# Output projection in segment 3 instead of segment 4 of every step, and ScalarE's copy of p ahead of its copy of k in odd steps

## The chip, the cores and the metric

The kernel runs on one core of a Trainium2 chip. The metric is the device time of one execution in microseconds (us); lower is better. TensorE is called PE, and PEld is its weight load; VectorE is DVE, ScalarE is ACT, GpSimd is POOL and SyncE is SP. SP issues all the DMAs.

## What is computed

One transformer layer on x of shape 16 x 512 x 256 in float32: x = x + attention(layernorm(x)), then x = x + ffn(layernorm(x)).

```python
qkv = inputs @ W_qkv                        # 256 -> 2048 (q), 1024 (k), 1024 (v)
# 32 query heads of 64, 16 key/value heads, each shared by two query heads
scores = einsum('bhqd,bhkd->bhqk', q, k) / 8 + slope[h] * (k_pos - q_pos)
attn = softmax(where(q_pos >= k_pos, scores, -inf))
out = einsum('bhqk,bhkd->bhqd', attn, v).reshape(B, S, 2048) @ W_out
# ffn, low rank: 256 -> 64 -> 1024, gelu, 1024 -> 64 -> 256
P = x @ U1;  H = gelu(P @ V1 + b1);  Q = H @ U2;  y = Q @ V2 + b2
```

## The kernel before

**Precision.** Each operand of a large product is kept as two float16 parts, a high and a low half, and a product is three matmuls (`split_mm`, L547). ACT writes most high halves (function `copy`, L812), DVE most low halves (`low`, L984), POOL the low half of p and of o (L1284, L1303).

**Passes, steps, segments.** The batch has 16 sequences. Each engine runs one instruction stream over passes i = 0 to 17 (modes FIRST for 0, MID for 1 to 15, LAST and TAIL for the emptying of the pipeline). A pass has 16 steps s, one for each key/value head, and a step has 5 segments n. The work is a software pipeline: in step s of a pass, q and k are projected for head s, the row maxima are taken for head s - 2, scores and exponentials belong to head s - 7, the attention products to head s - 8, and the rows of o of head s - 9 are transposed. So pass i still finishes sequence i in the first half of the steps of pass i + 1.

**PE, in each segment, in program order** (loop at L757 on): `scores(s, n)`; in four steps of a pass the FFN's `ffn_h`; `max_scores(s, n)`; in segments (15, 3) and (15, 4) the transposes of the next x; in segment 0 of odd steps the projection of k; in segment 4 the output projection `project_out` (L672); in segment 1 (even steps) or 2 (odd steps, and step 0) the projection of q; in segments 1 and 3 one of the two attention products, `attend(s, 0)` and `attend(s, 1)`, "the first" and "the second product" in what follows; in segment 4 of steps 0 to 3 and 8 to 11 the projection of v; and smaller pieces of the FFN. PE starts its operations in this order. Two PSUM banks serve the scores, so `scores(s, n)` waits for the exponential of two segments before, and two serve the maxima.

**The output projection.** o_t has room for 8 heads and is read in groups of 4 heads. Steps 12 to 15 project heads 0 to 3 (128 tokens in each step), steps 0 to 3 heads 4 to 7, steps 4 to 7 heads 8 to 11, steps 8 to 11 heads 12 to 15. Each is 12 matmuls of 128x128 by 256 columns. At the first step of a group (12, 0, 4, 8) `project_out` waits for the transposes of all its four heads. The last of those is issued by SP in that same step: SP waits for `lo_o`, which POOL gives at L1303 in segment 0, after ACT's `o_hi_lo` copy (in segment 0, behind the exponential of that segment and, where there is one, the copy of v), which waits for DVE's `o_f` (L1100) from the second product of the step before.

```python
def project_out(s):
    group, t = out_use(s)
    bank = next_proj(("out", s), acc_done, 16 * i + s - OUT_LAG + 1)
    if t == 0:
        for slot in range(2):
            pe.wait_ge(ot_in[slot], at(16 * (8 * i + (s - OUT_LAG) // 2 + 2)))
```

**DVE** adds the projected rows in `residual(s)` (L1053; the instruction is L1050), in the same segment as `project_out`; in steps 8 to 11 `statistics(s)` of the second layernorm follows. In segments 1 and 3 `normalise` (L1095, L1100) comes near the end of the segment's work.

**ACT** takes in segment n the copy of p of segment n - 1 (`high_p`, "the copy of p"), then the exponential of segment n (L862), and then the rest: v, o, maxima, k (`high_k`, L875) in segment 0 of odd steps, and layernorm pieces. In segment 1 of steps 13, 15, 1 and 3 it also computes two GELUs (L964), with a table load before and after them.

**PSUM banks of the projections.** Three banks are handed out in turn over the uses listed by `projection_order()`; `next_proj` makes PE wait until the use of three places before has been read.

Of the kernel before, what the change touches and what calls it, by code (L numbers as in the profile page):

```python
# [32 lines left out]
T = S // P  # L33
# [31 lines left out]
MAX_SEG, K_SEG, V_SEG, O_SEG = 2, 0, 4, 4  # L65
# [5 lines left out]
OUT_RING, OUT_GROUP, OUT_LAG, OUT_SEG = 8, 4, 12, 4  # L71
# [44 lines left out]
    return divmod(SEG * s + n - lag, SEG)  # L116


def q_segment(s):

    return 2 if s % 2 or s == 0 else 1
# [21 lines left out]
def projection_order():  # L143

    uses = []
    for s in range(KV):
        for n in range(SEG):
            if (s, n) in H_PAIRS:
                uses += [("h", 2 * H_PAIRS[s, n]), ("h", 2 * H_PAIRS[s, n] + 1)]
            if n == MAX_SEG and s % 4 == 2:  # L150
                uses.append(("max", s))
            if (s, n) in X_PAIRS:
                uses.append(("x", X_PAIRS[s, n]))
            if n == K_SEG and s % 2 == 1:
                uses.append(("k", s))
            if n == OUT_SEG:
                uses.append(("out", s))
            if (s, n) in LN2_T_AT:
                uses.append(("ln2", LN2_T_AT[s, n]))
            if n == q_segment(s):  # L160
                uses.append(("q", s))
                if s in SKIP_BANK:
                    uses.append(("skip", s))
            if n == V_SEG and s % 8 < 4:
                uses.append(("v", s))
            if (s, n) in U1_AT:
                uses.append(("p", U1_AT[s, n]))
            if (s, n) == Y_AT:
                uses += [("y", 0), ("y", 1)]
            if (s, n) in U2_PAIRS:  # L170
                uses.append(("u", U2_PAIRS[s, n]))
    return uses
# [12 lines left out]
FIRST, MID, LAST, TAIL = "first", "mid", "last", "tail"  # L185


def steps(mode):

    return range(STORE_AT + 1) if mode == TAIL else range(KV)  # L190
# [40 lines left out]
def out_in(mode, s):  # L231

    return mode in (FIRST, MID) if s >= OUT_LAG else mode in (MID, LAST)


def p_place(s, n):

    return (SEG * (s - ATT) + n) % P_RING


def in_stage(mode, s, lag):

    return s >= lag if mode == FIRST else s < lag if mode == LAST else mode == MID


def layer(nc, x, w_qkv, w_out, u1, v1, b1, u2, v2, b2, k_aug, q_aug, ident_d, ident_b_d, causal_d, out):
    B = x.shape[0]
    ctx = ExitStack()
    with ctx:
# [141 lines left out]
        def ffn_batch(i, s):  # L391

            return i - 1 if s >= 8 else i - 2

        def ffn_in(i, s):

            return 0 <= ffn_batch(i, s).value() < B
# [5 lines left out]
        def h_pairs(i, s):  # L403
            return {} if not ffn_in(i, s) else END_H_PAIRS if at_end(ffn_batch(i, s)) else H_PAIRS
# [4 lines left out]
        def u2_pairs(i, s):  # L409
            return {} if not ffn_in(i, s) else END_U2_PAIRS if at_end(ffn_batch(i, s)) else U2_PAIRS  # L410
# [126 lines left out]
        def _(pe):  # L537
# [30 lines left out]
            def body(i, mode):  # L568
# [189 lines left out]
                for s in steps(mode):  # L758
                    if mode == FIRST and s == 2:

                        pe.wait_ge(k_rows, 2)
                    if mode == FIRST and s == 6:
                        pe.wait_ge(const_in, 64)
                    if mode == FIRST and s == 8:
                        pe.wait_ge(set_done, 1)
                    if mode == FIRST and s == OUT_LAG:
                        pe.wait_ge(wo_lo, 2)
                    for n in range(SEG):
                        if in_stage(mode, s, ATT):
                            scores(s, n)  # L770
                        if (s, n) in h_pairs(i, s):
                            ffn_h(ffn_batch(i, s), h_pairs(i, s)[s, n])
                        if n == MAX_SEG and s % 4 == 2 and in_stage(mode, s, 6):
                            transpose_max(s)
                        if in_stage(mode, s, 2):
                            max_scores(s, n)
                        if (s, n) in X_PAIRS and mode in (FIRST, MID):
                            pair = X_PAIRS[s, n]
                            next_proj(("x", pair), lo_ln1, 2 * (i + 1) + pair + 1)
                            transpose_x(i + 1, pair)  # L780
                        if n == K_SEG and s % 2 == 1 and mode in (FIRST, MID):
                            pair = (s - 1) // 2
                            project(next_proj(("k", s), lo_k, i * (KV // 2) + pair + 1), QD + pair * P, pe_k)
                        if n == OUT_SEG and mode == LAST and s == OUT_LAG - T:
                            project_out_end()
                        elif n == OUT_SEG and out_in(mode, s) and not (mode == LAST and s > OUT_LAG - T):
                            project_out(s)
                        if n == q_segment(s) and mode in (FIRST, MID):
                            if s == 0:
                                pe.wait_ge(lo_ln1, at(2 * (i + 1)))  # L790
                            project(next_proj(("q", s), lo_q, i * KV + s + 1), s * P, pe_q)
                        if n in (1, 3) and in_stage(mode, s, ATT + 1):
                            attend(s, n // 2)
                        if (s, n) in LN2_T_AT and mode != FIRST:
                            transpose_x2(LN2_T_AT[s, n])
                        if n == V_SEG and s % 8 < 4 and mode in (FIRST, MID):
                            project_v(s)
                        if (s, n) in U1_AT and mode != FIRST:
                            ffn_p(U1_AT[s, n])
                        if (s, n) == Y_AT and ffn_in(i, s):  # L800
                            ffn_y(ffn_batch(i, s), 0)
                            ffn_y(ffn_batch(i, s), 1)
                        if (s, n) in u2_pairs(i, s):
                            ffn_u2(ffn_batch(i, s), u2_pairs(i, s)[s, n])
# [5 lines left out]
        def _(act):  # L810
# [41 lines left out]
            def body(i, mode):  # L852
# [11 lines left out]
                def high_p(s, n):  # L864
                    a = i * KV + s - ATT
                    if (s % KV, n) in POOL_MASKS:
                        act.wait_ge(masked, mask_count(i, s, n))
                    else:
                        act.wait_ge(exp_done, at(SEG * a + n + 1))

                    if 2 * a + AV_BEFORE[n] > 0:
                        act.wait_ge(pe_av, at(2 * a + AV_BEFORE[n]))
                    copy(p_hi[:, p_place(s, n), :], p_f[:, n, :]).then_inc(hi_p, 1)

                def high_k(s):  # L875
                    act.wait_ge(pe_k, at(i * (KV // 2) + (s + 1) // 2))
                    landed = K_DMAS * 16 * (2 * i + (s - 3) // RING + 1)
                    if landed > 0:
                        act.wait_ge(kdup_in[(s - 3) % RING // 2], at(landed))
                    copy(ks[0][:, :], proj("k", s)[:, :], KV_OUT).then_inc(hi_k, 1)  # L880
# [9 lines left out]
                for s in steps(mode):  # L890
# [4 lines left out]
                    for n in range(SEG):  # L895
# [4 lines left out]

                        if n > 0 and in_stage(mode, s, ATT):
                            high_p(s, n - 1)
                        if n == 0 and in_stage(mode, s, ATT + 1):
                            high_p(s - 1, SEG - 1)
                        if before(s, n, PP_LAG) in U1_AT and mode != FIRST:
# [28 lines left out]
                        if n == MAX_SEG and s % 4 == 2 and in_stage(mode, s, 6):  # L934
# [4 lines left out]
                            if 32 * (2 * i + q4 // 2 + 1) > 0:  # L939
                                act.wait_ge(m_in[q4 % 2], at(32 * (2 * i + q4 // 2 + 1)))  # L940
                            copy(mt[0][:, :], proj("max", s)[0:8 * T, 0:P], -1.0).then_inc(hi_m, 1)
                        if n == K_SEG and s % 2 == 1 and mode in (FIRST, MID):
                            high_k(s)
                        if (s, n) in LN1_AT and mode in (FIRST, MID):
                            t = LN1_AT[s, n]
                            if t == 0:
# [34 lines left out]
        def _(dve):  # L981
# [46 lines left out]
            def body(i, mode):  # L1028
# [75 lines left out]
                for s in steps(mode):  # L1104
# [3 lines left out]
                    for n in range(SEG):  # L1108
# [27 lines left out]
                        if n == q_segment(s) + q_lag(s) and mode in (FIRST, MID):  # L1136
                            dve.wait_ge(hi_q, at(g + 1))
                            low(qs[1][:, s % 2, :], proj("q", s)[:, :], qs[0][:, s % 2, :], Q_OUT).then_inc(lo_q, 1)
                        if n == OUT_SEG and out_in(mode, s):
                            if mode == LAST and s >= OUT_LAG - T:  # L1140
                                if s == OUT_LAG - T:
                                    dve.wait_ge(acc_done, at(16 * i - T))
                                    for k in range(T):
                                        residual(s + k)
                                    for k in range(T):
                                        statistics(s + k)
                            else:
                                residual(s)
                                if s in range(OUT_LAG - T, OUT_LAG) and mode != FIRST:
                                    statistics(s)  # L1150
# [233 lines left out]
```

## Time and profile before

| | |
|---|---|
| median of 3 runs | 2745.33 us (2740.84 to 2749.11) |
| profiled execution, its time | 2744.49 us |
| its span in the trace | 2742.5 us |
| mean granted TensorE clock | 0.989 |
| PE busy | 96% |
| POOL, ACT, DVE busy | 79%, 78%, 74% |

The span is what the trace covers, from the first to the last instruction; the time of the execution lies 2 us above it. In the stretch between the first and the last pass the schedule repeats every 165 us, once for each sequence. Times within the trace are counted from the start of the span.

### The profile page before, as it was taken

Reading aid. Unit: us, or ns where it says so; the run is one execution under the profiler, and the core shown is the slowest. Engines: PE = TensorE matmul, PEld = TensorE weight load, DVE = VectorE, ACT = ScalarE, POOL = GpSimd, SP = SyncE. Lnnn points to the kernel's source line nnn. Section 1 sums busy time; section 2 is a strip of 40 time slices with the busy share of each in tenths; the row PEclk is TensorE's granted clock in tenths of the full one; section 3 lists DMA queues with packets and bytes.
Section 4 is the critical chain, followed back from the end, with each engine's and each line's share of the span. In section 5 each row is a group of like instructions: output and inputs, shape, how many; then the busy total and the mean of one; then the engine's idle time right before and its main releaser. Section 6 shows DMA issues by size and latency. Waiting matters only on the chain.

```text
span 2742.5 us, 83206 instructions
## 1 busy us (share of the span) xinstructions
PE 2634.9 (96%) x30344; PEld 1797.7 (66%) x30344; DVE 2033.6 (74%) x6857; ACT 2142.4 (78%) x3856; POOL 2170.4 (79%) x2221
## 2 busy tenths in 40 slices
PE   5999999999999999999999999999999999999985
PEld 2666666666666667666666666666666666666663
DVE  5677777777777778777787777778777787777753
ACT  4777878778787887878778788877878778787883
POOL 4878788787877878788887887878788787887884
PEclk8999999999999999999999999999999999999997
DMA  6444444444445445444444444444444444444421
GB/s 182 100 98 96 97 95 93 96 94 93 98 91 105 93 89 103 95 94 97 96 94 94 95 92 98 98 92 95 94 102 94 93 101 89 99 96 95 99 46 32
DMA packets 489112, 260.75 MB, mean 95 GB/s; under 512 B 310064, under 2 KB 485168, under 8 KB 488704
## 3 DMA queue, kind: packets, MB, share of 16 engines
q1 hardware_dynamic: 488704, 255.44, 44.8%
q8 instruction: 241, 3.95, 0.6%
q14 instruction: 167, 1.37, 0.2%
HBM read 27.73 MB, written 8.39 MB: 13 GB/s over the span
## 4 chain that ended last, share of the span: by engine, by line
PE 68%; ACT 11%; issue 9%; POOL 5%; DVE 3%; DMA 2%; SPq 1%; ACTq 0%; POOLq 0%; DVEq 0%
PE proj L544 33%; PE scores L544 16%; PE o_acc L544 11%; PE max_scores L544 7%; ACT p_f L862 3%; ACT L862 3%; POOL p_lo L1284 3%; ACT p_hi L812 2%; ACT h_f L964 2%; POOL o_hi_lo L1303 1%; DMA o_t<-o_hi_lo 1%; DMA q_operands<-neg_max_t_lo 1%; POOL p_f L1278 1%; DVE max_scores L1043 1%; POOL h_lo L1289 1%
## 5 line engine op out<-in xcount | busy, mean ns | idle before, releaser
L1284 POOL TENSOR_TENSOR p_lo<-p_f,p_hi 128x512 f16<-128x512 f32 x1280 | 1477.4, 1164 | 249.5 <-ACT p_hi L812 248.0
L1043 DVE CUSTOM_DVE_ANT_0 max_scores<-max_scores,causal 128x512 f32<-128x512 f32 (+3 forms) x2048 | 971.4, 506 | 238.8 <-PE max_scores L544 201.7
L812 ACT ACTIVATE p_hi<-p_f 128x512 f16<-128x512 f32 x1280 | 804.7, 629 | 208.3 <-POOL p_f L1278 197.2
L862 ACT ACTIVATE p_f<-scores 128x512 f32<-128x512 f32 x1280 | 756.5, 591 | 176.0 <-PE scores L544 146.0
L544 PE MATMUL scores<-q_operands,k_lo_hi 128*128 128x512 f16 (+3 forms) x2048 | 607.5, 300 | 32.8 <-ACT p_f L862 26.1
L544 PE MATMUL scores<-q_operands,k_hi_aug 128*128 128x512 f16 (+3 forms) x2048 | 565.2, 299 | 0.0
L544 PE MATMUL o_acc<-v_hi_one,p_lo 128*128 128x65 f16 x5120 | 517.5, 194 | 15.7 <-POOL p_lo L1284 12.4
L544 PE MATMUL o_acc<-v_hi_one,p_hi 128*128 128x65 f16 x5120 | 517.0, 194 | 0.0
L544 PE MATMUL o_acc<-v_lo,p_hi 128*128 128x64 f16 x5120 | 516.4, 193 | 0.0
L544 PE MATMUL max_scores<-k_hi_aug,q_operands 96*128 96x512 f16 (+3 forms) x2048 | 492.1, 302 | 14.0 <-DMA k_lo_hi<-k_pair_lo 9.0
L544 PEld LDWEIGHTS o_acc<-v_hi_one,p_lo 128*128 128x128 f16 x5120 | 470.5, 98 | 50.5 <-POOL p_lo L1284 25.1
L544 PEld LDWEIGHTS o_acc<-v_lo,p_hi 128*128 128x128 f16 x5120 | 468.1, 98 | 39.5
L544 PEld LDWEIGHTS o_acc<-v_hi_one,p_hi 128*128 128x128 f16 x5120 | 467.4, 97 | 0.0
L1303 POOL TENSOR_TENSOR o_hi_lo<-o_f,o_hi_lo 128x512 f16<-128x512 f32 x256 | 296.9, 1160 | 171.3 <-ACT o_hi_lo L812 171.3
L544 PE MATMUL proj<-wo_hi,o_t 128*128 128x256 f16 x2016 | 372.7, 273 | 5.1 <-DMA o_t<-o_hi_lo 5.1
L544 PE MATMUL proj<-xn_t_hi,wqkv_lo 128*128 128x512 f16 x768 | 294.5, 383 | 3.2 <-DVE k_pair_lo L984 1.7
L544 PE MATMUL proj<-xn_t_lo,wqkv_hi 128*128 128x512 f16 x768 | 293.9, 383 | 0.0
L544 PE MATMUL proj<-xn_t_hi,wqkv_hi 128*128 128x512 f16 x768 | 293.8, 383 | 0.0
L544 PEld LDWEIGHTS scores<-q_operands,k_lo_hi 128*128 128x128 f16 x2048 | 199.8, 98 | 134.9 <-ACT p_f L862 35.1
L1043 DVE DVE_READ_ACCUMULATOR2_ANT row_max<- 128x1 f32 x2048 | 282.1, 138 | 1.3
L544 PE MATMUL scores<-ident_bf,causal 128*128 128x128 bf16 x1280 | 280.3, 219 | 0.0
L544 PE MATMUL proj<-wo_lo,o_t 128*128 128x256 f16 x1008 | 274.8, 273 | 0.0
(134 smaller groups left out, 4409.4 us busy)
## 6 DMA issues: line engine op xcount, KB each, us to landing
q_operands<-q_pair_hi SPq DMA_DIRECT2D x512, 128.0 KB, 2.5
q_operands<-q_pair_lo SPq DMA_DIRECT2D x512, 64.0 KB, 2.0
k_hi_aug<-k_pair_hi SPq DMA_DIRECT2D x256, 64.0 KB, 2.0
k_lo_hi<-k_pair_hi SPq DMA_DIRECT2D x256, 64.0 KB, 2.0
k_lo_hi<-k_pair_lo SPq DMA_DIRECT2D x256, 64.0 KB, 2.0
x_rows<-in_L_attn_inputs SPq DMA_DIRECT2D x17, 512.0 KB, 4.1
x_acc<-in_L_attn_inputs SPq DMA_DIRECT2D x64, 128.0 KB, 2.4
out<-x_rows SPq DMA_DIRECT2D x16, 512.0 KB, 3.4
```

The costliest lines, as they stand in the source:

```text
L544: return nc.tensor.matmul(out_ap, lhs, rhs, start=start, stop=stop, skip_group_check=True)
L812: return nc.scalar.activation(out_ap, in_ap, ACT.Copy, scale=scale)
L862: nc.scalar.activation(p_f[:, n, :], score_bank[(SEG * s + n) % 2][:, :], ACT.Exp).then_inc(exp_done, 1)
L964: nc.scalar.activation(h_f[:, c % 2, :], h_place(f, c)[:, :], ACT.Gelu_apprx_tanh, bias=b1c[:, c:c + 1], scale=1.0 / FFN_SCALE).then_inc(g ...
L1043: last = nc.vector.tensor_tensor_reduce(out=bank, in0=bank, in1=causal[:, (T - 1 - qt) * P:S], scale=1.0, scalar=-3e38, op0=ALU.add, op1=A ...
L1278: nc.gpsimd.affine_select(both, both, [[0, 2], [1, P]], ALU.is_ge, 0.0, base=0, channel_multiplier=-1).then_inc(masked, 1)
L1284: nc.gpsimd.tensor_tensor(p_lo[:, place, :], p_f[:, n, :], p_hi[:, place, :], ALU.subtract).then_inc(lo_p, 1)
L1289: nc.gpsimd.tensor_tensor(h_lo[:, c % 2, :], h_f[:, c % 2, :], h_hi[:, c % 2, :], ALU.subtract).then_inc(lo_h, 1)
L1303: nc.gpsimd.tensor_tensor(o_hl[:, slot, 1, :], o_f[:, slot, :, :].rearrange("p t c -> p (t c)"), o_hl[:, slot, 0, :], ALU.subtract).then_i ...
```

## The change

`OUT_SEG` is 4, and a new function `out_segment(s)` gives 3 for every step. PE's order and DVE's (`residual`, `statistics`) both take it, and so does the list from which the PSUM banks of the projections are handed out. Within segment 3, PE's code has the output projection ahead of the attention product, and DVE's has `residual` ahead of `normalise`. On ACT `high_k` moves from the end of segment 0 to segment 1, behind the copy of p that opens that segment and ahead of its exponential.

```diff
--- before.py
+++ after.py
@@ -116,6 +116,11 @@
     return divmod(SEG * s + n - lag, SEG)
 
 
+def out_segment(s):
+
+    return OUT_SEG - 1
+
+
 def q_segment(s):
 
     return 2 if s % 2 or s == 0 else 1
@@ -153,7 +158,7 @@
                 uses.append(("x", X_PAIRS[s, n]))
             if n == K_SEG and s % 2 == 1:
                 uses.append(("k", s))
-            if n == OUT_SEG:
+            if n == out_segment(s):
                 uses.append(("out", s))
             if (s, n) in LN2_T_AT:
                 uses.append(("ln2", LN2_T_AT[s, n]))
@@ -781,9 +786,9 @@
                         if n == K_SEG and s % 2 == 1 and mode in (FIRST, MID):
                             pair = (s - 1) // 2
                             project(next_proj(("k", s), lo_k, i * (KV // 2) + pair + 1), QD + pair * P, pe_k)
-                        if n == OUT_SEG and mode == LAST and s == OUT_LAG - T:
+                        if n == out_segment(s) and mode == LAST and s == OUT_LAG - T:
                             project_out_end()
-                        elif n == OUT_SEG and out_in(mode, s) and not (mode == LAST and s > OUT_LAG - T):
+                        elif n == out_segment(s) and out_in(mode, s) and not (mode == LAST and s > OUT_LAG - T):
                             project_out(s)
                         if n == q_segment(s) and mode in (FIRST, MID):
                             if s == 0:
@@ -900,6 +905,8 @@
 
                         if n > 0 and in_stage(mode, s, ATT):
                             high_p(s, n - 1)
+                        if n == K_SEG + 1 and s % 2 == 1 and mode in (FIRST, MID):
+                            high_k(s)
                         if n == 0 and in_stage(mode, s, ATT + 1):
                             high_p(s - 1, SEG - 1)
                         if before(s, n, PP_LAG) in U1_AT and mode != FIRST:
@@ -939,8 +946,6 @@
                             if 32 * (2 * i + q4 // 2 + 1) > 0:
                                 act.wait_ge(m_in[q4 % 2], at(32 * (2 * i + q4 // 2 + 1)))
                             copy(mt[0][:, :], proj("max", s)[0:8 * T, 0:P], -1.0).then_inc(hi_m, 1)
-                        if n == K_SEG and s % 2 == 1 and mode in (FIRST, MID):
-                            high_k(s)
                         if (s, n) in LN1_AT and mode in (FIRST, MID):
                             t = LN1_AT[s, n]
                             if t == 0:
@@ -1136,7 +1141,7 @@
                         if n == q_segment(s) + q_lag(s) and mode in (FIRST, MID):
                             dve.wait_ge(hi_q, at(g + 1))
                             low(qs[1][:, s % 2, :], proj("q", s)[:, :], qs[0][:, s % 2, :], Q_OUT).then_inc(lo_q, 1)
-                        if n == OUT_SEG and out_in(mode, s):
+                        if n == out_segment(s) and out_in(mode, s):
                             if mode == LAST and s >= OUT_LAG - T:
                                 if s == OUT_LAG - T:
                                     dve.wait_ge(acc_done, at(16 * i - T))
```

## Rows read from the trace of the kernel before

**Rows 1.** The profile's page, part 1: busy us, share of the span, instructions.
```profile
PE 2634.9 (96%) x30344; PEld 1797.7 (66%) x30344; DVE 2033.6 (74%) x6857; ACT 2142.4 (78%) x3856; POOL 2170.4 (79%) x2221
```

**Rows 2.** Waits, 440 to 2420 us, of PE and PEld: total us, times, longest.
```profile
PEld scores L544 <- ACT p_f L862: 23.6, 48, 0.6
...
PE scores L544 <- ACT p_f L862: 17.2, 36, 0.5
...
PE proj L544 <- DMA o_t<-o_hi_lo: 3.8, 4, 1.3
...
PE o_acc L544 <- POOL p_lo L1284: 3.4, 12, 0.3
```

**Rows 3.** Timeline, step 8: start us, us, engine, line, operation, out<-in, [idle before <-releaser].
```profile
1384.71 0.62 ACT L812 ACTIVATE o_hi_lo<-o_f 128x512 f16<-128x512 f32 x1
...
1385.41 1.16 POOL L1303 TENSOR_TENSOR o_hi_lo<-o_f,o_hi_lo 128x512 f16<-128x512 f32 x1 [0.72 <-ACT o_hi_lo L812]
...
1386.65 1.25 SPq L488 DMA_TRANSPOSE o_t<-o_hi_lo  x1
...
1388.46 0.19 PE L544 MATMUL o_acc<-v_hi_one,p_lo 128*128 128x65 f16 x1
...
1389.37 0.27 PE L544 MATMUL scores<-q_operands,k_lo_hi 128*128 128x256 f16 x1
...
1390.03 0.27 PE L544 MATMUL proj<-wo_hi,o_t 128*128 128x256 f16 x1
...
1391.34 0.38 PE L544 MATMUL proj<-wqkv_hi,xn_t_lo 128*128 128x512 f16 x1
```

**Rows 4.** Tile o_t over the whole span: time from issue to landing.
```profile
DMA to landing us min/median/max: 3.0/3.1/6.5
```

**Rows 5.** Timeline at step 4 of the second pass: a transpose, and the projection behind it.
```profile
195.41 1.24 SPq L488 DMA_TRANSPOSE o_t<-o_hi_lo  x1
...
198.72 0.27 PE L544 MATMUL proj<-wo_hi,o_t 128*128 128x256 f16 x1 [0.28 <-DMA o_t<-o_hi_lo]
```

**Rows 6.** Tile o_t, window 195 to 200 us: that transpose's landing.
```profile
DMA to landing us min/median/max: 3.2/3.2/3.2
```

**Rows 7.** Timeline: transpose issue and start of second product, steps 0, 4, 12, 12.
```profile
1304.11 1.25 SPq L488 DMA_TRANSPOSE o_t<-o_hi_lo  x1
...
1306.73 0.19 PE L544 MATMUL o_acc<-v_hi_one,p_lo 128*128 128x65 f16 x1
...
1349.97 1.24 SPq L488 DMA_TRANSPOSE o_t<-o_hi_lo  x1
...
1351.27 0.19 PE L544 MATMUL o_acc<-v_hi_one,p_lo 128*128 128x65 f16 x1
...
1428.74 1.26 SPq L488 DMA_TRANSPOSE o_t<-o_hi_lo  x1
...
1430.27 0.19 PE L544 MATMUL o_acc<-v_hi_one,p_lo 128*128 128x65 f16 x1
...
2586.18 1.26 SPq L488 DMA_TRANSPOSE o_t<-o_hi_lo  x1
...
2587.71 0.19 PE L544 MATMUL o_acc<-v_hi_one,p_lo 128*128 128x65 f16 x1
```

**Rows 8.** Timeline of GELU steps 15 and 3: ScalarE's k, second product, next scores.
```profile
1291.75 0.60 ACT L812 ACTIVATE k_pair_hi<-proj 128x512 f16<-128x512 f32 x1 [0.40 <-PE proj L544]
...
1297.31 0.19 PE L544 MATMUL o_acc<-v_hi_one,p_lo 128*128 128x65 f16 x1
...
1298.42 0.28 PE L544 MATMUL scores<-q_operands,k_lo_hi 128*128 128x256 f16 x1
...
1341.41 0.20 PE L544 MATMUL o_acc<-v_hi_one,p_lo 128*128 128x65 f16 x1
...
1342.96 0.28 PE L544 MATMUL scores<-q_operands,k_lo_hi 128*128 128x256 f16 x1 [0.47 <-ACT p_f L862]
```

**Rows 9.** Timeline, step 0: the first product behind step 15's last p.
```profile
1302.95 0.20 PE L544 MATMUL o_acc<-v_hi_one,p_lo 128*128 128x65 f16 x1 [0.28 <-POOL p_lo L1284]
```

## The prediction

> **What bounds the kernel.** I read the page first: PE is busy 96% of the span, the others at most 79% [rows 1]. So the time changes by what PE does more, or waits more. Then the waits of PE over twelve repetitions (440 to 2420 us), to see what interrupts it: scores wait for the exponential 36 times as matmuls and 48 times as weight loads, three and four times a sequence; the output projection waits for the transposes 4 times in all; the first product waits for p's low half 12 times, once a sequence [rows 2]. PE has little idle time to win, and its order is nearly free of waits because each operand arrives just before its use. The question is what the new order wins at the first kind of wait and loses at the second. For that I read the timeline around single steps.
>
> **The move costs no PE work.** In step 8 the second product starts at 1388.46, the next scores at 1389.37, the output projection at 1390.03 and the projection of v at 1391.34 [rows 3]. So the product takes 0.91 us of PE's time and the projection 1.31 us. After the change the projection starts where the product starts now, and the product and the scores of segment 4 come 1.31 us later; from segment 4's end on the order is the old one. The same 12 matmuls, the same DVE additions and the same DMAs are issued; only waits change.
>
> **What it wins: the GELU steps.** In step 3 the scores behind the second product start 1.55 us after it (1341.41 to 1342.96), against 0.91 us in step 8: 0.64 us lost, put down to ACT, which is late by its table loads [rows 3, 8]. Steps 1 and 13 show the same (these are the 36 waits of matmuls, three a sequence [rows 2]). In step 15 the distance is 1.11 us (1297.31 to 1298.42), 0.20 us lost [rows 8]. The projection, 1.31 us ahead of the product, gives ACT that much more time and covers all four: 3 x 0.64 + 0.20 = 2.12 us a sequence.
>
> **What it costs: the first step of each group.** In steps 12, 0, 4 and 8 the projection needs a transpose issued in that very step. From issue to landing the median is 3.1 us [rows 4]. One place shows the whole wait: issued at 195.41, landed 3.2 us later [rows 6], that is at 198.61, and PE's projection starts at 198.72 with the DMA as its releaser [rows 5]. So PE starts about 0.1 us after landing, or 3.2 us after the issue in the usual case. In step 8 the issue is at 1386.65: operands are usable at 1389.85, and the projection starts at 1390.03, 0.18 us later, without a wait [rows 3]. The new place is 1388.46, which is 1.39 us too early. In the same way [rows 7]:
> - step 12: 1428.74 + 3.2 - 1430.27 = 1.67 us short
> - step 4: 1349.97 + 3.2 - 1351.27 = 1.90 us
> - step 0: 1304.11 + 3.2 - 1306.73 = 0.58 us
>
> Together 5.54 us a sequence. The pattern is the same in every sequence: the last step 12 has the issue 1.53 us ahead of the product (2586.18 and 2587.71), as the one at 1428.74 has [rows 7]. Does the issue move with the change? It hangs on ACT's copy of o (1384.71), then on POOL (1385.41, 1.16 us), then SP at 1386.65 [rows 3]. That copy stands behind the exponential of segment 0, and this one follows scores(s, 0), ahead of which PE has done the same work as before. So the issue keeps its distance to PE's schedule, where ACT is ready. The wait cannot hide behind the product any more, since PE takes its matmuls in order: what stands behind the waiting projection is the second product, then segment 4, and everyone who waits for them (DVE's normalise, ACT's exponential).
>
> **Chain behind the later scores.** The scores of segment 4 come 1.31 us later, and the path from them over exponential, copy of p and POOL's low half to the next step's first product loses the projection as cover. The same path from the scores of segment 3 does not. Three places:
> - Step 7 into step 8: no projection of v stands between, so ACT reaches the exponential of segment 0 and the copy of o later. The copies on ACT and the subtraction on POOL cost 0.62 and 1.16 us [rows 3]. I take 0.5 us on the issue in step 8; the bounds are 0 (ACT has slack) and 1.31 us (the whole shift).
> - Step 15 into step 0: the first product already waits 0.28 us for p's low half [rows 9], and DVE has the x copies to do behind a normalise that comes 1.31 us later. I take 0.3 us, bounds 0 and 1.31 us.
> - The other steps without a v projection (4 to 6 and 12 to 14) have a projection of q or k, another 1.31 us (the same 6 x 512 columns as v's), in between. I take 0.2 us in all; bounds -0.3 us (the present waits of this kind, one a sequence, might go [rows 2]) and 1.5 us.
>
> That is 1.0 us a sequence.
>
> **The k part.** ACT's copy of k waits for PE's k projection for 0.40 us in step 15 [rows 8]; the copy of p now runs in that time, and p's low half and the exponential of segment 1 get up to 0.4 us earlier. In other odd steps k's high half is later by up to one copy, 0.62 us [rows 3], and so are DVE's low half and SP's six k DMAs behind it, and on SP the odd step's transpose. Their reader is max_scores of the next step, a whole step after the k projection, and that work is its cover; in odd steps no group of the output projection starts. On PE I cost it at nothing: it is not PE's wait. Without that cover it would be 0.6 us in eight steps, 5 us a sequence. A gain is possible only through ACT's lateness in GELU steps, which the projection already covers.
>
> **The bank rotation** changes with the order. I went through the 78 uses: each waits for the use three places before, and nowhere is that a use which is read after the place where PE now asks for it. The closest are the projections of steps 13, 15, 1 and 3 behind a GELU, which is over before the second product. Nothing.
>
> **A rule against the row.** The wait rests on 3.1 us from issue to landing [rows 4]. The Trainium skill, page "DMA: Bandwidth & Descriptors", section "Anatomy of one DMA", gives a DMA a fixed cost of about 2.0 us, of the software-issued kind. As an estimate by that page, the sum would come out near no change (the second rival below). The trace does not agree, since its median for this transpose is 3.1 us.
>
> **The sum.** Per sequence: 5.54 + 1.0 - 2.12 = 4.42 us. Fifteen passes have all of it: 66.3 us. The first pass has one group start (step 12), 1.67 us. The pass that empties the pipeline has two (steps 0 and 4), and its PE is less loaded; I take 3 us, bounds 0 and 6. Together 71 us, on the profiled execution's 2744.5 us: 2815 us. That execution is 0.8 us below the median of the runs, which changes nothing here.
>
> **Rivals.**
> 1. *The waits are not there, the GELU gain is* (faster). If ACT reached the copy of o earlier in steps 12, 0, 4 and 8, the issue could come before PE needs it. What decides is whether the four waits sum to less than about 1.1 us a sequence. Then 15 x 2.12 = 32 us are won: 2713 us. For it: the GELU waits are real, 36 of them [rows 2]. Against it: the issues would have to come 1.4 to 1.9 us earlier in three steps, and their origin is PE's own scores in segment 0. Chance 0.05.
> 2. *Landing is quicker for the early reader, by 1.1 us* (no change). The four shortfalls would be 0.57, 0.80, 0.29 and 0 us, 1.66 in all; 1.66 + 1.0 - 2.12 = 0.54 us a sequence, 8 us, and with the ends 2755 us. (The Trainium skill's page "DMA: Bandwidth & Descriptors" would have it so.) Against: the minimum of all 256 landings is 3.0 us [rows 4]. Together with other ways in which shortfall and gain meet, chance 0.05.
> 3. *The chain behind the scores of segment 4 becomes the bound in all steps without v* (slower still). If eight steps lose 0.5 us each in place of my 0.2 in all, 3.8 us a sequence more: 57 us, 2872 us. For it: POOL and ACT are near 80% busy [rows 1]. Against: the q or k projection of 1.31 us still stands there. Chance 0.15.
>
> The forecast itself has 0.75. A measurement of this kernel can tell about 0.3%, 8 us, from no change. Forecast and rival 3 are slower, 0.90; rival 2 is the same, 0.05; rival 1 faster, 0.05. **Range.** With waits at 5.14 (no 0.1 us of start) and no chain term: 3.0 us a sequence, 2744.5 + 45 + 2 = 2792; a little below that if the issue moves up with ACT's relief, 2778. Up: chain terms of 3 us a sequence give 6.4, which is 96 + 5 us: 2846; I take 2850. This leaves out most of rival 3, and rivals 1 and 2.
>
> **What the profile after would show.** PE waiting for the o_t DMA four times a sequence in place of 4 times in twelve sequences, by 0.5 to 2 us, with PE's projection 3.2 us behind SP's issue in steps 12, 0, 4, 8; the waits of scores on the exponential in the GELU steps gone; the schedule repeating every 169 to 170 us in place of 165 ((2586.18 - 1428.74) / 7 [rows 7]). The forecast is wrong if the output projection of these steps starts without a wait, if GELU waits stay, or if the first product's waits for p's low half grow past 1 us a sequence.

## The result and the profile after

| | before | after |
|---|---|---|
| median of the runs | 2743.41 us (4 runs) | 2853.58 us (4 runs, 2848.98 to 2861.01) |
| ratio | | 1.0398, 95% interval 1.0383 to 1.0413 |
| span of the profiled execution | 2742.5 us | 2847.0 us |
| PE busy | 2634.9 us, 96% | 2643.6 us, 93% |
| mean granted TensorE clock | 0.989 | 0.989 |

The change costs 110 us, 4.0%. The direction was forecast; the size was forecast as 71 us, with 2850 us as the end of the range. The time lies 3.6 us above that end.

The page of the kernel after: part 1, then part 4, the chain that ended last, by engine and by line.

```profile
PE 2643.6 (93%) x30344; PEld 1791.6 (63%) x30344; DVE 2105.6 (74%) x6857; ACT 2128.0 (75%) x3856; POOL 2179.8 (77%) x2221
...
PE 69%; POOL 8%; DMA 8%; ACT 7%; issue 5%; DVE 3%; SPq 1%; ACTq 0%; POOLq 0%; DVEq 0%
...
PE proj L549 34%; PE scores L549 15%; PE o_acc L549 13%; DMA o_t<-o_hi_lo 7%; PE max_scores L549 6%; POOL p_lo L1289 4%; POOL o_hi_lo L1308 3%; ACT p_f L867 2%; ACT p_hi L817 1%; ACT o_hi_lo L817 1%; ACT L867 1%; DVE x_rows L1182 1%; PE proj L711 1%; ACT h_f L969 1%; DVE max_scores L1048 0%
```

PE is busy for about as long as before (8.7 us more) and the span of the profiled execution is 104.5 us longer: the time went into PE's waits. The DMA of o_t is 7% of the chain now; it was 1% before.

The waits of PE and PEld from 440 to 2420 us (total us, times, longest), as in [rows 2]:

```profile
PEld max_scores L549 <- DVE row_max L1048: 24.9, 57, 0.8
...
PEld scores L549 <- ACT p_f L867: 9.2, 33, 0.3
...
PE proj L549 <- DMA o_t<-o_hi_lo: 62.1, 46, 1.9
...
PE proj L549 <- DVE q_pair_lo L989: 15.2, 11, 1.4
...
PE max_scores L549 <- DVE row_max L1048: 8.8, 23, 0.4
...
PE o_acc L549 <- POOL p_lo L1289: 5.2, 11, 0.5
...
PE proj L549 <- DVE x2n_t_lo L989: 3.0, 12, 0.3
```

The stretch holds twelve sequences before and eleven and a half after. The projection waits for the transposes 46 times in place of 4. The scores wait for the exponential 33 times by at most 0.3 us as weight loads, and no more as matmuls; before it was 48 times by up to 0.6 us, and 36 of these as matmuls. Three more kinds of wait are new or grown. The projection waits 11 times for VectorE's low half of q, once a sequence and by 1.4 us each, which was not there before. A product of the FFN waits once a sequence for VectorE's `x2n_t_lo`, 0.3 us. And the maxima's products wait for VectorE: 57 weight loads do, but only 23 matmuls. Where a weight load alone waits, PE still has matmuls to finish, so the row of the matmuls, 8.8 us, is the one that counts as time of PE. The kernel before has no row of max_scores matmuls waiting for VectorE, and this one of weight loads:

```profile
PEld max_scores L544 <- DVE row_max L1043: 6.5, 24, 0.3
```

Timeline of the kernel after at the four group starts, steps 4, 8, 12 and 0: SP's transpose, PE's last max_scores ahead of the projection, and the projection.

```profile
1398.43 1.24 SPq L493 DMA_TRANSPOSE o_t<-o_hi_lo  x1
...
1399.53 0.38 PE L549 MATMUL max_scores<-k_hi_aug,q_operands 96*128 96x512 f16 x1
...
1401.63 0.27 PE L549 MATMUL proj<-wo_hi,o_t 128*128 128x256 f16 x1 [1.72 <-DMA o_t<-o_hi_lo]
...
1440.00 1.25 SPq L493 DMA_TRANSPOSE o_t<-o_hi_lo  x1
...
1441.13 0.38 PE L549 MATMUL max_scores<-k_hi_aug,q_operands 96*128 96x512 f16 x1
...
1443.21 0.27 PE L549 MATMUL proj<-wo_hi,o_t 128*128 128x256 f16 x1 [1.70 <-DMA o_t<-o_hi_lo]
...
1483.46 1.26 SPq L493 DMA_TRANSPOSE o_t<-o_hi_lo  x1
...
1484.77 0.38 PE L549 MATMUL max_scores<-k_hi_aug,q_operands 96*128 96x512 f16 x1
...
1486.70 0.27 PE L549 MATMUL proj<-wo_hi,o_t 128*128 128x256 f16 x1 [1.55 <-DMA o_t<-o_hi_lo]
...
1524.76 1.25 SPq L493 DMA_TRANSPOSE o_t<-o_hi_lo  x1
...
1527.15 0.38 PE L549 MATMUL max_scores<-k_hi_aug,q_operands 96*128 96x512 f16 x1
...
1527.96 0.27 PE L549 MATMUL proj<-wo_hi,o_t 128*128 128x256 f16 x1 [0.43 <-DMA o_t<-o_hi_lo]
```

The projection starts 3.20, 3.21, 3.24 and 3.20 us after the issue. The max_scores block ahead of it takes 0.22 us of PE (512 columns: the distance from one such matmul to the next), so PE stood 1.88, 1.86, 1.71 and 0.59 us: 6.04 us a sequence. Over all sequences the medians are 1.89, 1.85, 1.70 and 0.59 us.

Timeline of step 6, PE and DVE; the first line is the same place one sequence earlier:

```profile
1252.42 0.28 PE L549 MATMUL proj<-wo_hi,o_t 128*128 128x256 f16 x1 [1.38 <-DVE q_pair_lo L989]
...
1422.10 0.38 PE L549 MATMUL max_scores<-k_hi_aug,q_operands 96*128 96x512 f16 x1
...
1423.13 0.67 DVE L989 SCALAR_TENSOR_TENSOR q_pair_lo<-proj,q_pair_hi 128x512 f16<-128x512 f32 x1
...
1423.86 0.28 PE L549 MATMUL proj<-wo_hi,o_t 128*128 128x256 f16 x1 [1.38 <-DVE q_pair_lo L989]
```

PE is through with the maxima at 1422.32 and starts the projection at 1423.86, 1.54 us later, when VectorE's `q_pair_lo` of this step is done. The projection does not read q; it is given the PSUM bank that q has just had. The distance from 1252.42 to 1423.86 is one period of the new schedule: 171.4 us, against 165.3 us between the issues of [rows 7]. Over fifteen periods, from the maxima's transpose in step 2 of the second pass to that of the pass that empties the pipeline, the mean is 171.2 us (179.01 to 2747.25 in the trace after) against 164.6 us (175.79 to 2645.16 before): 6.6 us more a sequence, 98.9 us of the 104.5.

Timeline of GELU step 3 after, second product and next scores:

```profile
1391.85 0.19 PE L549 MATMUL o_acc<-v_hi_one,p_lo 128*128 128x65 f16 x1
...
1392.76 0.27 PE L549 MATMUL scores<-q_operands,k_lo_hi 128*128 128x256 f16 x1
```

0.91 us, where it was 1.55 us [rows 8]: the GELU wait is gone.

### The profile page after: what moved, and what is told of

It is laid out like the page before. It is cut to its first block, busy times and chain, and to the rows that moved or that the text cites. A ratio compares the mean times of both kernels' runs of the same rounds, so it can differ in the third digit from the quotient of the medians.

```text
span 2847.0 us, 83206 instructions
## 1 busy us (share of the span) xinstructions
PE 2643.6 (93%) x30344; PEld 1791.6 (63%) x30344; DVE 2105.6 (74%) x6857; ACT 2128.0 (75%) x3856; POOL 2179.8 (77%) x2221
## 4 chain that ended last, share of the span: by engine, by line
PE 69%; POOL 8%; DMA 8%; ACT 7%; issue 5%; DVE 3%; SPq 1%; ACTq 0%; POOLq 0%; DVEq 0%
PE proj L549 34%; PE scores L549 15%; PE o_acc L549 13%; DMA o_t<-o_hi_lo 7%; PE max_scores L549 6%; POOL p_lo L1289 4%; POOL o_hi_lo L1308 3%; ACT p_f L867 2%; ACT p_hi L817 1%; ACT o_hi_lo L817 1%; ACT L867 1%; DVE x_rows L1182 1%; PE proj L711 1%; ACT h_f L969 1%; DVE max_scores L1048 0%
## 5 line engine op out<-in xcount | busy, mean ns | idle before, releaser
L1283 POOL TENSOR_SCALAR_AFFINE_SELECT p_f<-p_f 128x256 f32<-128x256 f32 x384 | 157.4, 410 | 207.4 <-ACT p_f L867 201.9
L549 PEld LDWEIGHTS proj<-wo_hi,o_t 128*128 128x128 f16 x2016 | 196.5, 97 | 152.3 <-issue 105.1
```

The source lines that it names most:

```text
L549: return nc.tensor.matmul(out_ap, lhs, rhs, start=start, stop=stop, skip_group_check=True)
L1283: nc.gpsimd.affine_select(both, both, [[0, 2], [1, P]], ALU.is_ge, 0.0, base=0, channel_multiplier=-1).then_inc(masked, 1)
```

## The experiments

Two theories stood against each other. The first: the loss is the sum of single waits at places that can be named (the transposes at the four group starts, the bank in step 6, VectorE's maxima behind steps 5 and 15), less the GELU waits. The second: the loss is the lost cover between the scores of segment 4 and the next step's first product, in every step that moves, and PE's waits only stand where that lateness shows. Each kernel is timed together with the kernel before on its own chip, and the ratios are to that one. The medians of the kernel before differ by up to 4 us between the chips (2743.41 to 2747.50 us), so a few us between runs of different chips say little; e1 to e4 share a chip, e5 to e8 another, e9 and e10 a third.

### e1: the output projection alone

```diff
-                        if n == K_SEG + 1 and s % 2 == 1 and mode in (FIRST, MID):
-                            high_k(s)
                         if n == 0 and in_stage(mode, s, ATT + 1):
                             high_p(s - 1, SEG - 1)
...
+                        if n == K_SEG and s % 2 == 1 and mode in (FIRST, MID):
+                            high_k(s)
                         if (s, n) in LN1_AT and mode in (FIRST, MID):
```

> The output projection moves in all sixteen steps, ScalarE's copy of k stays where it was before. Theory (waits for the transposes 6.0 us a sequence, a bank wait of 1.5 us in step 6, some chain cost, less 2.1 us of GELU waits): the k part is worth nothing on PE, so 2853 us within 5 us. Rival (the later copy of k makes VectorE late, and that is the part of the loss that the prediction lacked, 30 to 40 us): about 2815 to 2825 us.

Measured: 2861.86 us, ratio 1.0410 (1.0393 to 1.0427). That is 4 us above the end of what was expected (2858 us), and far from the rival's. The interval overlaps the whole change's (1.0383 to 1.0413), so inside the whole change the k part is worth nothing that these times tell from zero, and it is not the missing loss. The trace does show a small share of it: with the projection alone one wait of a scores matmul a sequence is left, which the whole change does not have.

```profile
PE scores L549 <- ACT p_f L867: 3.2, 12, 0.3
```

### e2: the k part alone

```diff
 def out_segment(s):
 
-    return OUT_SEG - 1
+    return OUT_SEG
```

> Only ScalarE's copy of p goes ahead of its copy of k; the output projection stays in segment 4. Theory: no PE wait is added, and the four GELU waits of a sequence (0.64 us three times, 0.20 us) can shrink by at most the 0.40 us that the copy of p now hides, so 2725 to 2743 us. Rival (k arrives late for VectorE and the DMAs): slower than 2750 us.

Measured: 2718.04 us, ratio 0.9894 (0.9878 to 0.9909): 29 us faster, 7 us below what was expected. The waits, weight loads of the scores from 440 to 2420 us:

```profile
PEld scores L549 <- ACT p_f L867: 2.3, 13, 0.2
```

13 in place of 48. The timeline of its step 3, ACT's copy of k, PE's second product and the next scores:

```profile
1484.86 0.59 ACT L817 ACTIVATE k_pair_hi<-proj 128x512 f16<-128x512 f32 x1
...
1489.96 0.19 PE L549 MATMUL o_acc<-v_hi_one,p_lo 128*128 128x65 f16 x1
...
1491.00 0.28 PE L549 MATMUL scores<-q_operands,k_lo_hi 128*128 128x256 f16 x1
```

From product to scores is 1.04 us, 0.13 us over 0.91, where it was 0.64 us over. So 0.51 us is won in such a step: the 0.40 us that ACT waited for PE, and 0.1 us that the expectation did not count. Read in every sequence, the median distance is 1.04 to 1.05 us in steps 13, 1 and 3 (it was 1.55 us), and 0.92 us in step 15 (it was 1.11 us), so 1.7 us a sequence are won, 27 us in sixteen. The k part, costed at nothing on PE, is nearly the whole of what the kernel can win; with the projection moved it only has less to win, because the projection covers the same waits.

### e3: another bank in step 6

```diff
             if n == q_segment(s):
+                if s == 6:
+                    uses.append(("skip", s))
                 uses.append(("q", s))
-                if s in SKIP_BANK:
+                if s in SKIP_BANK[1:]:
                     uses.append(("skip", s))
```

> The whole change, but the unused place of step 6 in the rotation of the PSUM banks stands ahead of q's use and not behind it, so that step 6's output projection gets a bank other than the one q has just had. Theory: the wait of 1.54 us a sequence on VectorE's low half of q is gone, fifteen to sixteen times, 23 us less: about 2830 us. Rival (VectorE and ScalarE are late there in any case, and PE waits for something else a little later): no difference, 2850 us or more.

Measured: 2835.64 us, ratio 1.0321 (1.0305 to 1.0336): 18 us less than the whole change (21 us by the ratios, the two having run on different chips), where 23 us were expected. Waits of PEld and PE from 440 to 2420 us:

```profile
PEld max_scores L551 <- DVE row_max L1050: 25.2, 58, 0.8
...
PE proj L551 <- DMA o_t<-o_hi_lo: 64.3, 47, 2.4
```

There is no row of the projection waiting for `q_pair_lo` any more, and the waits for the transposes are a little longer (64.3 us against 62.1 us). So the bank wait was real and most of it additional. It does not come from a shifted rotation: in the list of uses of the kernel before, step 6's projection stands three places behind q of step 6 too, and has the same bank. There it came a segment later, when VectorE had read q. It is the earlier start that meets the reader, and another rotation is a remedy.

### e4: the group starts stay in segment 4

```diff
 def out_segment(s):
 
-    return OUT_SEG - 1
+    return OUT_SEG if s % OUT_GROUP == 0 else OUT_SEG - 1
```

This is on e3's rotation.

> As the run with the other bank rotation, but the first step of each group of the output projection (12, 0, 4, 8) keeps it in segment 4; the other twelve steps have it in segment 3. Theory: all waits for the transposes are gone, the GELU gain of 2.1 us a sequence stays, a chain cost of 0 to 0.5 us a sequence remains: 2712 to 2722 us, faster than the kernel before. Rival (the loss is the lost cover between the scores of segment 4 and the next first product, in every step): 12 of 16 steps keep it, so slower than the kernel before, 2770 us or more.

Measured: 2732.26 us, ratio 0.9947 (0.9932 to 0.9961). With twelve of sixteen steps moved the kernel is faster than before, so the second theory falls as the main cause: 103 us between e3 and e4 belong to the four group starts. But it is 10 us above the end of the expected range and 14 us slower than e2, which moves none. (e4 also has the other rotation, which no run has alone.) Waits of PEld and PE from 440 to 2420 us:

```profile
PEld max_scores L551 <- DVE row_max L1050: 26.1, 60, 0.8
...
PE max_scores L551 <- DVE row_max L1050: 9.2, 24, 0.4
...
PE proj L551 <- DMA o_t<-o_hi_lo: 4.1, 6, 1.5
```

The transposes are back at a few waits, and the maxima wait as much as after the whole change; e2 has no such row of matmuls. The row is two waits and 0.8 us a sequence, most of the 14 us. Where they wait is seen in the timeline of the kernel after behind step 5, DVE and PE:

```profile
1415.30 1.35 DVE L1182 SCALAR_TENSOR_TENSOR x_rows<-proj,x_rows 128x512 f32<-128x512 f32 x2 [0.44 <-PE proj L549]
...
1417.66 0.33 DVE L1048 CUSTOM_DVE_ANT_0 max_scores<-max_scores,causal 128x128 f32<-128x128 f32 x1
...
1418.10 0.39 PE L549 MATMUL max_scores<-k_hi_aug,q_operands 96*128 96x384 f16 x2 [0.33 <-DVE row_max L1048]
```

In step 5 DVE adds y (two instructions, 1415.30 to 1416.65) and normalises only after that; its maxima of segment 4 end at 1417.99, and PE's max_scores that needs their bank starts at 1418.10. PE has come to it early, because the projection that used to stand between is now ahead. The other such wait of a sequence is behind step 15.

### e5: steps 5 and 15 stay too

```diff
-    return OUT_SEG if s % OUT_GROUP == 0 else OUT_SEG - 1
+    return OUT_SEG if s % OUT_GROUP == 0 or s in (5, 15) else OUT_SEG - 1
```

> As e4, and steps 5 and 15 keep the output projection in segment 4 too; ten steps have it in segment 3. Theory: the only wait that e4 added beside e2 is PE's maxima of the next step waiting for VectorE, behind steps 5 (its y additions) and 15 (its x copies), 1.1 us a sequence; without it 17 us less than e4: 2712 to 2718 us. Rival (a cost spread over all the steps whose later scores lose the cover): at most 4 us less than e4, 2728 us or more.

Measured: 2722.47 us, ratio 0.9913 (0.9897 to 0.9930), 10 us less than e4, between the two expectations.

```profile
PEld max_scores L551 <- DVE row_max L1050: 12.9, 49, 0.3
...
PE proj L551 <- DMA o_t<-o_hi_lo: 8.1, 9, 1.8
```

The 24 waits of the maxima's matmuls are gone with the two steps: e5 has no such row. Of the weight loads 49 short waits are left, against 24 before the change, and no matmul waits behind them. So the two steps carry all that the maxima cost PE. The profile also has 9 waits for the transposes where e4 and e2 have 6, so it happened to catch more late landings (8.1 us, 5.5 us in e2), and the first product waits 3.3 us for p's low half (0.9 us in e2). That is room for the 4 us by which e5 stays above e2; whether they come from the other ten steps, from chance or from the rotation is not shown.

### e6: only the group starts move

```diff
-    return OUT_SEG - 1
+    return OUT_SEG - 1 if s % OUT_GROUP == 0 else OUT_SEG
```

> Only the four group starts (steps 12, 0, 4, 8) have the output projection in segment 3, with ScalarE's k behind p as in e2. Theory: four waits for the transposes, 6.0 us a sequence on e2's 2718 us: 2805 to 2815 us. Rival (the waits only take the place of others): less than 40 us on e2, under 2760 us.

Measured: 2822.70 us, ratio 1.0277 (1.0256 to 1.0299), 105 us above e2 and 8 us above the end of the expected range. Waits from 440 to 2420 us, then one of its steps 8:

```profile
PE proj L549 <- DMA o_t<-o_hi_lo: 66.3, 47, 2.7
...
PE o_acc L549 <- POOL p_lo L1289: 5.7, 12, 0.5
...
PE proj L549 <- DVE x2n_t_lo L989: 3.1, 12, 0.3
```

```profile
1255.76 1.25 SPq L493 DMA_TRANSPOSE o_t<-o_hi_lo  x1
...
1257.36 0.38 PE L549 MATMUL max_scores<-k_hi_aug,q_operands 96*128 96x512 f16 x1
...
1258.97 0.27 PE L549 MATMUL proj<-wo_hi,o_t 128*128 128x256 f16 x1 [1.24 <-DMA o_t<-o_hi_lo]
```

Four steps of a sequence carry the loss. Two waits come along with them: the first product's for p's low half, by up to 0.5 us where e2's are at most 0.2 us, and that of the FFN product for `x2n_t_lo`, 0.3 us. Both are in the whole change too.

In this step 8 PE stood 1.39 us, not 1.86 us: step 7 has its projection in segment 4 here. So the half us on the issue in step 8 does come from the move in step 7. Read over all sequences, PE stands 1.90, 1.40, 1.70 and 0.87 us in steps 4, 8, 12 and 0. In step 0 that is 0.3 us more than after the whole change: with k behind p the first product no longer waits 0.28 us there [rows 9], so PE is earlier against the issue.

### e7: the copy of o first

In the four group starts only: on ACT the block of the o copy ahead of `high_p(s - 1, 4)`, on POOL the subtraction for o ahead of `low_p(s - 1, 4)`; on e3's rotation.

```diff
@@ ACT, segment 0
+                        if segment == O_SEG and in_stage(mode, s, ATT + 2) and s % OUT_GROUP == 0:
+                            ...
+                            copy(o_hl[:, slot, 0, :], ...).then_inc(hi_o, 1)
                         if n > 0 and in_stage(mode, s, ATT):
                             high_p(s, n - 1)
@@ POOL, segment 0
+                        if n == 0 and in_stage(mode, s, ATT + 2) and s % OUT_GROUP == 0:
+                            ...
                         if n == 0 and in_stage(mode, s, ATT + 1):
                             low_p(s - 1, SEG - 1)
```

> As e3 (whole change, other bank rotation), but in steps 12, 0, 4 and 8 ScalarE copies o ahead of p's last copy and of the exponential of segment 0, and GpSimd takes o's low half ahead of p's, so that the transpose can be issued earlier. Theory (the issue hangs on the place of the copy of o behind PE's scores of segment 0): the issue comes 2 us or more earlier in its step, the waits for the transposes nearly vanish, some of it comes back as waits for p's low half: 2780 to 2810 us, against 2836 us. Rival (the issue is set by SyncE's queue or by the second product of the step before): waits as in e3, 2830 us or more.

Measured: 2766.98 us, ratio 1.0081 (1.0066 to 1.0096): 69 us less than e3, 13 us below the range expected. Waits from 440 to 2420 us, then one of its steps 8:

```profile
PE o_acc L551 <- POOL p_lo L1303: 24.1, 36, 1.0
...
PE proj L551 <- DMA o_t<-o_hi_lo: 1.3, 1, 1.3
```

```profile
1232.52 1.25 SPq L495 DMA_TRANSPOSE o_t<-o_hi_lo  x1
...
1235.84 0.27 PE L551 MATMUL proj<-wo_hi,o_t 128*128 128x256 f16 x1
```

The projection comes 3.32 us after the issue and does not wait. In e3 PE was ready 1.35 us after the issue in this step, so the issue is 2.0 us earlier against PE; in the other three starts it is 2.0 to 2.3 us.

One wait for the transposes is left of 47, and p's low half is waited for 36 times (11 in e3), by up to 1.0 us. So the issue of the transpose did hang on the place of the o copy behind PE's scores of segment 0, as the prediction had it. The engines' time that o now takes first is time that p's low half comes later; the long wait for the transposes became a shorter one of the first product.

### e8, e9, e10: what is left to win

```diff
-    return OUT_SEG - 1
+    return OUT_SEG - 1 if s in (1, 3, 13) else OUT_SEG
```

> Only steps 1, 3 and 13 have the output projection in segment 3, with ScalarE's k behind p as in e2. Theory: e2 still has GELU waits of 0.14, 0.14 and 0.27 us in these steps, they go and nothing comes: 0 to 9 us less than e2, 2709 to 2718 us. Rival (the later scores cost in every step that moves): 2722 us or more.

> The kernel of e2 once more, on the chip of e10: 2718 us within 5 us, 1.0% below the kernel before.

> The kernel of e8 once more, on the chip of e9. Theory (the rest of the GELU waits, 0.55 us a sequence, goes): 5 to 10 us below e9. Rival (the 8 us between e2 and e8 were two chips): within 3 us of e9.

Measured: e8 2709.46 us, ratio 0.9873 (0.9858 to 0.9888). On one chip together, e9 (the k part alone) 2715.82 us, 0.9893 (0.9878 to 0.9908), and e10 (the kernel of e8) 2711.14 us, 0.9879 (0.9862 to 0.9895). Waits of the weight loads of e8 from 440 to 2420 us:

```profile
PEld max_scores L549 <- DVE row_max L1048: 6.3, 25, 0.3
...
PEld scores L549 <- ACT p_f L867: 4.1, 13, 0.3
```

In the three steps the scores now follow the product by 0.90 to 0.91 us, so the 0.13 to 0.15 us that e2 still lost in each, 0.4 us a sequence, are gone. The weight loads of the maxima wait 25 times in place of e2's 12 (2.9 us there), and one scores matmul waits for VectorE, 0.7 us. The medians differ by 5 to 9 us in both comparisons, in the direction expected, but the intervals overlap; that e8 is faster than e2 is likely and not settled. Both are more than 1% faster than the kernel before, and 5% faster than the change.

## Why the prediction was wrong in size

**Right, and to 0.05 us.** *PE starts 3.2 us after the issue*: 3.20 to 3.24 us. *The four shortfalls, 1.67, 1.90, 1.39 and 0.58 us, and 0.5 us on the issue in step 8*: 1.71, 1.88, 1.86 and 0.59 us; 6.04 us forecast and 6.04 us found. *The issue keeps its distance to PE's schedule*: it does, and e7 shows why. *The GELU waits are covered*: no wait of a scores matmul on the exponential is left between 440 and 2420 us, though the projection alone leaves one of 0.3 us a sequence (e1). Two of the agreements owe something to luck. The 0.5 us was picked between bounds of 0 and 1.31 us; e6 confirms its cause and gives 0.47 us as its size (1.86 less 1.39). And in step 0 two shifts that were not forecast, of 0.3 us each, cancel: the k part takes 0.28 us of PE's wait away and so brings PE nearer to the issue (0.87 us short in e6), and the move of the other steps gives it back (0.59 us). The direction, the places and the largest term of the sum stand.

**The step that failed: the bank rotation.** "I went through the 78 uses ... Nothing." That was wrong for one use. Step 6's projection has its bank three places behind q of the same step: q (segment 1), the unused place, the maxima (segment 2), then the projection. VectorE reads q's bank only in segment 2 behind its maxima, and PE, with the projection moved up, asks for it 1.54 us before that. The bank is the one that this projection had before the change too, so the order of uses showed nothing new; only the time did. Fifteen or sixteen times that is 24 us; taking it away gave 18 us back (e3), 21 us by the ratios. The check went by the order of uses and by the segment, and did not lay the reader's time of finishing (1423.80) beside the time at which PE would come (1422.32).

**The chain term was too small as well.** I took 0.3 us behind step 15 and 0.2 us for the other steps without v, by ACT and POOL. The waits that grew are mostly of another engine: the matmuls of the maxima wait for VectorE 8.8 us in eleven and a half sequences where they did not wait before, 0.8 us a sequence, and the FFN product for `x2n_t_lo` 3.0 us, 0.3 us a sequence. The matmul waits for p's low half stayed at one a sequence (3.4 us [rows 2], then 5.2 us), 0.2 us a sequence more. Together 1.2 us, where 0.5 us were taken. Behind step 5 the projection was PE's work while VectorE added y, normalised and took its maxima. The prediction followed the later scores and left the later normalise, which stands ahead of VectorE's maxima, at one place only. Moving twelve steps without the starts costs 14 us (e4 against e2), and the steps 5 and 15 carry the larger part of it (e5).

**The sum again.** A sequence takes 6.6 us more (171.2 in place of 164.6 us, the means of fifteen periods); forecast were 4.42. The bank wait adds 1.54 us and brings it to 5.96, and the 0.7 us by which the chain term was too small to about 6.65. In the profiled executions the first pass and the end have 5.6 us, where 4.7 us were forecast. The places named so make up the whole loss, within some tenths of a us a sequence.

**The k part** was costed at nothing "on PE", with the gain limited to what the projection covers already. Inside the whole change that holds (e1). Alone it is worth 29 us (e2), and the forecast did not see that this half of the change was the good one, because it read the two halves only together.

**The rivals.** Landings were not quicker (the second), and the GELU gain did not come alone (the first). The third, lost cover as the bound in all steps without v, has its 57 us refuted by e4 and e5: it is 14 us for twelve steps.

**The fixed cost of a DMA.** This transpose lands 3.1 us after its issue in the median [rows 4], and after the change PE starts 3.20 to 3.24 us behind the issue at the group starts read. The Trainium skill's page "DMA: Bandwidth & Descriptors", section "Anatomy of one DMA", has about 2.0 us as the fixed cost of a DMA on the path that GpSimd issues, and adds the bytes moved, divided by 436 GB/s. SP issues this one, so the figure is of another path. The estimate by that page in the prediction also left the bytes out: with 256 KB they are 0.6 us more, and the second rival, which needs a landing 1.1 us quicker, is then not what the page would give. For this transpose the measurement decides.

## What to carry to other kernels

Before a consumer is moved earlier, lay its new start beside the arrival of each operand and the release of each buffer that it takes: at the places read, issue to start was constant to 0.05 us, and a shortfall so worked out came back as a wait of that size. Do the same with rotating buffers, by the time at which the reader finishes: step 6 kept its buffer, and only came for it 1.54 us too early. And cost each half of a two-part change by itself: here the reorder of two ACT copies won 1%, while the larger half lost 4%, nearly all of it in five steps of sixteen (the group starts and step 6).

## What was not expected

The placing of one short wait on ACT. Having the copy of p run while PE finishes k saves 0.51 us in a step whose wait was 0.40 us, three times a sequence, and 0.2 us in step 15. With 16 sequences this is most of the 29 us that e2 won, in a kernel in which ACT is busy 78% and PE 96%. The other surprise is e7: giving o precedence over p on two engines took nearly all of 47 waits away and cost 36 shorter ones, 69 us in balance.
